# Finer sum pieces, two helper buffers, and sums of group 1 of the second pass in a free bank, in a graph network kernel on one core

## What is computed

```python
# layer 0, a gated cell; layer 1, two neighbour means
msg = h[src] @ W_msg.T + b_msg + edge_embed[clip(edge_type)]
messages = segment_sum(msg, dst, num_segments=3125)
x = layernorm(x + gru_cell(messages, x, W_ih, W_hh, b_ih, b_hh))
def sage(h, w_self, w_neigh, b):
    neigh = segment_sum(h[src], dst) / maximum(deg, 1)
    return h @ w_self + neigh @ w_neigh + b
h = relu(sage(x, w_self1, w_neigh1, b1))
x = layernorm(x + sage(h, w_self2, w_neigh2, b2))
```

## Time and profile before

| | us |
|---|---|
| median of three runs | 766.2 |
| profiled execution, its own time | 764.69 |
| span of its instructions | 762.9 |
| counting stage, from the start of the tiles to the verdict | about 15 to 412 |
| first pass | about 414 to 516 |
| second pass | about 516 to 650 |
| third pass | about 650 to 763 |

### The profile page before, as it was taken

The page is one execution under the profiler, slowest core; times in us unless marked ns, Lnnn a source line. Parts: engine busy times, 40 slices in busy tenths (PEclk is TensorE's granted clock), DMA queues, the critical chain, the costliest instruction groups (busy, mean ns, idle before and its releaser), DMA issues.

```text
span 762.9 us, 14609 instructions
## 1 busy us (share of the span) xinstructions
PE 662.5 (87%) x3061; PEld 311.9 (41%) x3061; DVE 468.4 (61%) x1469; ACT 244.3 (32%) x486; POOL 171.0 (22%) x342
## 2 busy tenths in 40 slices
PE   2767899989888899888766999948999999999995
PEld 0222344434333343333222544413555456666663
DVE  7789999998888879999894357651010010034434
ACT  3044444332422235656664245531111221100000
POOL 2432333232222235445340012230100111100000
PEclk9879999999999999999998999989999999999998
DMA  5000000000000000000002011000100110211210
GB/s 155 1 1 0 1 1 1 0 1 0 1 0 1 0 1 1 0 1 0 0 0 81 16 28 55 16 30 29 42 25 17 41 41 29 87 43 43 69 31 16
DMA packets 29437, 17.32 MB, mean 23 GB/s; under 512 B 1841, under 2 KB 28223, under 8 KB 29400
## 3 DMA queue, kind: packets, MB, share of 16 engines
q1 hardware_dynamic: 29400, 16.82, 7.6%
HBM read 10.38 MB, written 6.44 MB: 22 GB/s over the span
## 4 chain that ended last, share of the span: by engine, by line
PE 64%; DVE 18%; issue 7%; DVEq 5%; ACT 2%; DMA 1%; SPq 0%; POOL 0%; ACTq 0%
PE PS L917 14%; PE PS L994 11%; PE PS L1232 11%; PE PS L873 10%; DVE S L619 10%; DVE D L613 3%; PE PS L1161 3%; PE PS L1055 2%; PE PS L1196 2%; DVEq L619 2%; PE PS L895 1%; PE PS L1150 1%; PE PS L1149 1%; PE PS L1028 1%; PE PS L1029 1%
## 5 line engine op out<-in xcount | busy, mean ns | idle before, releaser
L917 PE MATMUL PS<-S,D 128*128 128x449 bf16 x780 | 219.0, 368 | 53.8 <-DVE S L619 45.4
L619 DVE TENSOR_SCALAR S<-iota_h,src_col,src_w 128x440 bf16<-128x440 f16 x749 | 253.1, 399 | 0.2 <-issue 0.2
L472 POOL COPY S<-T 128x27 bf16 (+1 forms) x262 | 113.5, 434 | 236.4 <-PE PS L917 222.2
L917 PEld LDWEIGHTS PS<-S,D 128*128 128x128 bf16 x780 | 75.7, 97 | 193.6 <-DVE S L619 152.3
L1275 ACT ACTIVATE AT<-digits 128x1152 uint8 (+5 forms) x75 | 77.1, 1029 | 160.7 <-DVE digits L608 160.7
L613 DVE TENSOR_TENSOR D<-iota_t,dst 128x384 bf16<-128x384 f16 x260 | 93.8, 361 | 33.3 <-PE PS L917 32.1
L873 PE MATMUL PS<-AT,xp 128*128 128x512 bf16 x375 | 91.3, 379 | 0.0
L994 PE MATMUL PS<-AT,x1p 128*128 (+2 forms) x450 | 86.8, 353 | 0.0
L1232 PE MATMUL PS<-xp,AT 128*128 128x384 bf16 (+1 forms) x525 | 85.6, 326 | 0.0
L1232 PEld LDWEIGHTS PS<-xp,AT 128*128 (+2 forms) x525 | 51.5, 98 | 33.9 <-issue 0.3
L994 PEld LDWEIGHTS PS<-AT,x1p 128*128 128x128 bf16 x450 | 39.5, 99 | 44.0 <-issue 2.3
(11 more groups left out here) (167 smaller groups left out, 628.8 us busy)
## 6 DMA issues: line engine op xcount, KB each, us to landing
slot<-x_rows SPq DMA_DIRECT2D x12, 256.0 KB, 2.9
xstage<-x SPq DMA_DIRECT2D x6, 256.0 KB, 4.9
x_rows<-slot SPq DMA_DIRECT2D x6, 256.0 KB, 2.2
y_rows<-slot SPq DMA_DIRECT2D x6, 256.0 KB, 2.2
res_rows<-slot SPq DMA_DIRECT2D x6, 256.0 KB, 2.2
slot<-res_rows SPq DMA_DIRECT2D x6, 256.0 KB, 3.1
out_rows<-slot SPq DMA_DIRECT2D x6, 256.0 KB, 2.2
slot<-xT SPq DMA_DIRECT2D x3, 256.0 KB, 2.6
```

What stands on the lines that cost most here:

```text
L472: g.tensor_copy(S[:, where:where + V, SPAN:WIDE], T[:, :, ds(c0 + where, V)].rearrange("p k c -> p c k")).then_inc(sem("types_placed"), 1)
L619: v.tensor_scalar(S[:, u, 0:SPAN], iota_h[:, :], src_col[:, ds(c0 + u, 1)], src_w[:, ds(c0 + u, 1)], ALU.is_equal, ALU.mult).then_inc(sem( ...
L917: mm(PS[:, par, 0:WIDE], ring[:, u, :], S[:, u, 0:WIDE], start=opens and u == 0, stop=last).then_inc(sem("tiles_summed" if last else "item ...
```

## The change

Four things are changed.

1. `LEAST` becomes a table of five runs (2 for tiles 0 to 8, 3 for 9 to 15, 4 for 16 to 18, 5 for 19 to 22, 12 for 23 and 24; before: 2 up to tile 20, 4 from there). In `count_tile` the passes 1 to `LEAST - 2` are written out ahead of the loop, each with a piece between its halves and one behind it. So a tile has `2 * (LEAST - 2) + 3` pieces: 3, 5, 7, 9 and 23. The plan holds all 125 steps, so none is left behind the last tile.
2. `apart` has two halves that take turns (in rows 0 to 15 of the last tile's columns of `AT`, which are written later), and `last_rows` no longer waits for its own `Relu` at the end of each round.
3. `p2_second` sums group 1 of the second pass in PSUM bank 2: six row blocks ahead of `rows_back(6)`, the rest behind it and behind the rest of `p2_first`. What the first step of the second pass did between the shares of that sum is now written out ahead of `p2_step(2)`, and `second(0)` and `hidden(1)` stand inside `p2_step(2)`. `chunk_inputs(0)` uses bank 0. ACT and DVE have their parts in the same new order.
4. The DMA that brings group 0's rows back into `slot[2]` is issued in the first pass, ahead of the last store.

```diff
@@ constants
-PIECES = 3
-LEAST = 2
-LEAST_WIDE = 4
+LEAST_RUNS = ((0, 9, 2), (9, 16, 3), (16, 19, 4), (19, 23, 5), (23, 25, 12))
+LEAST = tuple(n for lo, hi, n in LEAST_RUNS for _ in range(lo, hi))
-EARLY_PLAN = (0,) * 7 + (4, 4, 5, 4, 5, 4, 5, 7, 5, 7, 7, 7, 8, 10, 9, 9, 10, 10)
+EARLY_PLAN = (0,) * 7 + (3, 3, 5, 3, 5, 3, 5, 6, 5, 6, 6, 6, 8, 9, 10, 11, 18, 13)
+    apart = AT[:, 0:16, (TILES - 1) * P:(TILES - 1) * P + SPAN // 8]
@@ SP, first pass
+                if q == NC:
+                    sp.wait_ge(sem("p1_y"), NC + 1)
+                    sp.wait_ge(sem("p1_x1_out"), 16)
+                    sp.dma_start(slot[2][:, :].rearrange("p (t f) -> p t f", f=F),
+                                 x1_dram[0:512, :].rearrange("(t p) f -> p t f", p=P)).then_inc(sem("p2_x1_in"), 16)
                 x1_store(q)
@@ PE, count_tile
                 early_piece(t, 0)
...
+                single = LEAST[t] - 2
+                pieces = 2 * single + 3
+                early_piece(t, 0, pieces)
+                for i in range(1, single + 1):
+                    one_pass(first + t + i, first + i, D, i - 2 if is_dense(t) and i >= 3 else None, between_halves=lambda: early_piece(t, 2 * i - 1, pieces))
+                    early_piece(t, 2 * i, pieces)
+                    if t == TILES - 1 and i == 2:
                         turn_tile(t - 1)
...
+                with pe.Fori(single + 1, more) as i:
+                    one_pass(first + t + i, first + i, D, i - 2 if is_dense(t) else None)
+                early_piece(t, pieces - 2, pieces)
+                one_pass(first + t + more, first + more, D, None, closes=True, between_halves=lambda: early_piece(t, pieces - 1, pieces))
@@ PE, end of the first pass
+                if q == NC:
+                    p2_second(0, 6)
                 rows_back(q)
+            p2_second(6, 20)
             p2_first(20, TILES - 1)
+            p2_second(20, TILES - 1)
@@ PE, second pass
+            p2_close(0)
             degrees(0, 512)
             chunk_inputs(0, 512)
+            p2_close(1)
+            hidden(0, 512)
+            degrees(1, 512)
+            chunk_inputs(1, 512)
...
+                if isinstance(q, int) and q == 2:
+                    agg("p2", x1p, q, w, [delayed, rest, lambda: second(1, 512)])
+                else:
+                    agg("p2", x1p, q, w, [inputs, lambda: None, lambda: second(q - 1, 512)])
@@ ACT, last_rows
-                    a.activation(apart[:, :], iota_h[:, :], ACT.Abs, scale=-1.0, bias=src_col[:, ds(c, 1)]).then_inc(sem(f"apart_set{t}"), 1)
+                    near = apart[:, ds((b & 1) * 8, 8), :]
+                    a.activation(near, iota_h[:, :].rearrange("p (a n) -> p a n", a=8), ACT.Abs, scale=-1.0,
+                                 bias=src_col[:, ds(c, 1)]).then_inc(sem(f"apart_set{t}"), 1)
...
-                    act.wait_ge(sem(f"S_last_set{t}"), i - 2)
```

More of the change, by code:

```diff
@@ L183, in graph_kernel @@
     src_w = place(r, "src_w", [P, CP], fp32)
-    apart = place(r, "apart", [P, SPAN], bf16)
     assert r[0] <= Z_at + 15 * F * 4
@@ L289, in second_rows, with sum_bank @@
             return PS[0:rows, 3:5, :].rearrange("p b (h w f) -> p (b h) w f", h=2, w=2)[:, 0:k, which, :]
+        def sum_bank(q):
+            return q + 1 if isinstance(q, int) and q < 2 else 0
         def s_at(q):
@@ L800, in mean_neighbours @@
                 dve.wait_ge(sem("p2_agg"), q + 1)
-                v.tensor_tensor(nT, nT, PS[:, 1 if isinstance(q, int) and q == 0 else 0, 0:w], ALU.mult).then_inc(sem("p2_n"), 1)
+                v.tensor_tensor(nT, nT, PS[:, sum_bank(q), 0:w], ALU.mult).then_inc(sem("p2_n"), 1)
             def residual(q, last):
@@ L812, in _ @@
             mean_neighbours(0, 512)
-            with dve.Fori(1, NC) as q:
+            mean_neighbours(1, 512)
+            residual(0, False)
+            with dve.Fori(2, NC) as q:
                 mean_neighbours(q, 512)
@@ L882, in early_steps, with early_piece @@
                         early_sum(q, j0, j1)
-            def early_piece(t, n):
-                pieces = PIECES + 2 if is_dense(t) else PIECES
+            def early_piece(t, n, pieces):
                 n0, steps = EARLY_BEGIN[t], EARLY_PLAN[t]
@@ L1093, in p2_first, with p2_second @@
                 pe.nop()
+            def p2_second(j0, j1):
+                pe.wait_ge(sem("p1_c"), NC + 1)
+                pe.wait_ge(sem("p1_low"), -(-j1 // 4))
+                with pe.If(general):
+                    pe.nop()
+                with pe.Else():
+                    for j in range(j0, j1):
+                        for s in range(PARTS):
+                            mm(PS[:, 2, :], x1p[:, j, s, :], AT[:, j, 512:1024], start=(j == 0 and s == 0), stop=False)
+                pe.nop()
             fills = {0: (lambda: late_sum(NC, 0, TILES), lambda: late_sum(NC - 1, 0, 4)),
@@ L1125, in chunk_inputs @@
             def chunk_inputs(q, w):
-                bank = 2 if isinstance(q, int) and q == 0 else 1
+                bank = 0 if isinstance(q, int) and q == 0 else 1
                 if bank == 1:
@@ L1180, in inputs, with delayed, rest @@
                     chunk_inputs(q, w)
-                agg("p2", x1p, q, w, [inputs, lambda: None, lambda: second(q - 1, 512)])
-            p2_step(1, 512)
-            with pe.Fori(2, NC) as q:
+                def delayed():
+                    second(0, 512)
+                    hidden(1, 512)
+                def rest():
+                    degrees(q, w)
+                    chunk_inputs(q, w)
+                if isinstance(q, int) and q == 2:
+                    agg("p2", x1p, q, w, [delayed, rest, lambda: second(1, 512)])
+                else:
+                    agg("p2", x1p, q, w, [inputs, lambda: None, lambda: second(q - 1, 512)])
+            p2_step(2, 512)
+            with pe.Fori(3, NC) as q:
                 p2_step(q, 512)
@@ L1461, in inputs_out @@
                 act.wait_ge(sem("p2_h_sum"), 2 * q)
-                a.activation(slot[3][:, 0:w], PS[:, 2 if isinstance(q, int) and q == 0 else 1, 0:w], ACT.Copy).then_inc(sem("p2_x1c"), 1)
+                a.activation(slot[3][:, 0:w], PS[:, 0 if isinstance(q, int) and q == 0 else 1, 0:w], ACT.Copy).then_inc(sem("p2_x1c"), 1)
             def relu_rows(q, w):
@@ L1480, in _ @@
             inputs_out(0, 512)
-            with act.Fori(1, NC) as q:
+            act.wait_ge(sem("p2_agg"), 1)
+            stage_sums("p2", 1)
+            relu_rows(0, 512)
+            inputs_out(1, 512)
+            second_out(0, False)
+            with act.Fori(2, NC) as q:
                 relu_rows(q - 1, 512)
```

46 lines of the change are left out of this document (16 added, 30 removed).

## The result

The changed kernel takes 735.75 us in the median of four runs (734.35 to 736.11), the kernel before, timed beside it, 766.59 us (four runs, 764.7 to 769.02): a ratio of 0.959 with a 95% interval of 0.956 to 0.962. The profiled execution has a span of 733.9 us, 29.0 less than before. The forecast was 733.9 us, with a range of 726 to 746.

What follows compares the result with a forecast made beforehand. The prediction took DVE to bound the counting stage and PE the second pass. Terms 18.8 + 4.4 + 3.1 + 6.0 = 32.3 us off the profiled 764.7 gave 732.4; 1.5 more for the median made 733.9, range 726 to 746.

Steps and rivals of the forecast that it cites:

- Finer pieces, tiles 9 to 23: Counting stage: nearly every piece cut to one step, so DVE waits less for PE; 18.8 us, bounds 9.4 and 27.8.
- ACT's helper, tile 24: Tile 24's helped batches: without ACT's wait for its own Relu, DVE sets the pace; 4.4 us, bounds 0 and 5.6.
- Behind the last tile: After tile 24: fifteen leftover matmuls go and the last pass ends earlier, so digits start sooner; 3.1 us, bounds 1.8 and 3.7.
- Group 1's sum in bank 2: Between the passes: 75 matmuls move from the second pass into PE's idle time; 6.0 us, bounds 3 and 8.4.
- The early load: Ahead of the second pass: loading slot[2] early removes a 1.95 us DMA wait, counted within the moved sum's 6.0 us.
- I leave 0.3 for each of the 20 changes from tile 4 on: Counting stage: DVE's wait for PE assumed to remain at each change from one tile to the next, 6.0 us in all.
- the 1 us that was named as the bound of being wrong: Tiles 21 to 23: waits of more than 1 us between written-out passes would make the prediction wrong.
- Slower: Counting stage: loading code for 37 more written-out passes holds PE and so DVE; up to 798 us, chance 0.03.
- Pieces only move the waits: Counting stage: PE is late in the written-out passes, gaining 9.4 us in place of 18.8; 743 us, chance 0.18.
- The helper loop isn't ACT's wait: Tile 24 keeps its 2.33 us round, as DVE, PE and ACT are locked in one ring; 737.5 us, chance 0.1.
- the moved sum gives little: Between the passes: new waits for DVE are longer than reckoned, gaining 3 us for 6; 737 us, chance 0.09.
- More than forecast: Counting stage: the waits left at the tiles' changes vanish as well; 727 us, chance 0.08.

Runs made afterwards that it cites:

- e9: Changed kernel with tile 20's digits moved to tile 23, spread steps, 18 plus six zero products, later ACT help in tile 24: 732.31 us, beside the unaltered changed kernel's 733.89.
- e1: Kernel before with only the LEAST table, written-out passes, new plan and finer pieces: 745.38 us, ratio 0.973.
- e4: Kernel before with only the LEAST table and written-out passes, pieces and plan as before: 765.85 us, ratio 0.9996.
- e11: Changed kernel with no steps around tile 23's closing pass, its 18 steps in the other 21 pieces: one time of 738.12 us.
- e6: Changed kernel with tile 20's digits taken at the start of tile 23 instead of in tile 22: 733.5 us, ratio 0.9605.
- e7: Changed kernel with another plan, 5, 5, 9 and 16 steps in tiles 10, 12, 22 and 23: 734.93 us, ratio 0.961.
- e2: Kernel before with only apart in two halves and no wait of ACT for its own Relu: 761.81 us, ratio 0.9945.
- e8: Changed kernel with the load of slot[2] back at its old place behind p1_done: one time of 733.9 us.
- e12: Changed kernel with ACT's help in tile 24 from the fourth batch on, DVE making the third's sixth row: 735.47 us, ratio 0.960.
- e3: Kernel before with only group 1's second-pass sum in bank 2 and the early load of slot[2]: 758.1 us, ratio 0.990.

## Why the prediction was right

Predicted 733.9, measured 735.75 and, beside e9, 733.89. That the second meets the forecast to the hundredth is luck. The gain in the medians was 30.8 and 30.9 us, and 29.0 between the first two profiled executions, where the sum says 32.3; and the 1.5 us that were added for the median over a profiled execution did not come (735.75 against 735.67). The terms of the sum, in us:

| term | predicted | measured |
|---|---|---|
| *Finer pieces, tiles 9 to 23* | 18.8 | 16.5 |
| *ACT's helper, tile 24* | 4.4 | 4.0 |
| *Behind the last tile* | 3.1 | 3.0 |
| *Group 1's sum in bank 2* and *The early load* | 6.0 | 7.3 |
| clock behind the last tile | not foreseen | -2.1, or 0 |
| up to tile 4, behind `hidden(1)` | not foreseen | 0.3 |

- **Finer pieces.** The mechanism is shown: e1 has it alone with the full 16.4 us, e4 has the same straight code without the finer pieces and gains nothing. What was mis-sized is "I leave 0.3 for each of the 20 changes from tile 4 on": the 21 starts of tiles 4 to 24 hold 9.3 us and not 6.0. At the starts of tiles 4 to 20, where DVE takes digits between `D_again` and its next `D`, 0.19 to 0.44 stay; tiles 23 and 24 have no digits there, and each keeps the 1.3 us that it had before. At tile 24 moving the steps takes nothing off it (e11), at tile 23 digits do (e6). Tiles 21 and 22 keep 0.77 and 0.63 at their starts, which no run explains. Inside tiles 21 to 23 another 1.6 us stay, where 3.0 were allowed for tiles 22 and 23. The largest, 0.88 in tile 22, is under the 1 us that was named as the bound of being wrong; it stands behind a piece of two steps in the middle of the tile, while the prediction says that at most the last piece of a tile has two, and e7 removes it with two steps fewer. Two of the signs did not come: DVE's waits are 12.2 us and not near 9, and the largest is 1.31 and not under 1.
- **ACT's helper.** The round fell to DVE's pace as foreseen, the form of 55 elements costs nothing, and ACT's late start stayed (1.31 us; 1.2 were left for it). But the 4.0 us are not the helper's alone: by itself it gives 2.3 (e2), the finer pieces by themselves 1.3 (e1), and 0.4 need both. The working took the span of fourteen helped batches as one rate; only the last eight ran at 2.33 us. So the size came out right in part by luck: the finer pieces removed other waits in the same tile, which the working had put on the helper.
- **Behind the last tile** is right in both its parts. 2.9 of the 3.0 us come with the finer pieces (e1).
- **Group 1's sum in bank 2.** The waits came as worked out: 0.27 for 0.45, and 1.17 for 1.2 (DVE's "1.85 in all" is 0.42 + 0.69 + 0.69 = 1.80, which takes 0.05 off both). Too high was "about 0.25 us each" for four new blocks with branches: the trace has no gap there. With that 1.0 and 0.2 the 5.8 of the working (of which "6.0" was made) come to 7.0, against 7.3. The early load, counted with them, gives nothing (e8). The 1.7 us for the clock depend on the execution: in e2 the second pass's first share ran in 5.99 us with the kernel's old order, the low clock having fallen on the matmuls ahead of it, and from the transposes of group 5 to `hidden(1)` it took 47.4 us where before had 49.2 and e4 50.1. So this term is 5 to 8 us, by which execution with the old order one takes.
- **The clock.** Not foreseen at all. Behind the last tile PE waits for the verdict, before and after (4.2 us), falls to the lower level in that wait and stays there for about 7 or about 14 us. The profile of before has 7, the changed kernel's first one 14 and its second 7, at 90.3 and 92.4 us from the verdict to group 5. Both lengths occur with either order: of the four profiled executions that end the counting stage as before, one has the long one (e4), and of the eight that end it as the change does and have no products, five (e1, the first profile after, e7, e11, e12). One and the same kernel shows both, so the length is not fixed by the order of work; whether the change makes the long one likelier, these few don't tell, and what sets it stays open.
- **The rivals.** *Slower*, by code loading, is out: e4 holds all written-out passes and has the time of before. The queue that brings instructions moved 28 packets, before 24, and the rows show no wait for it. The Trainium skill, "Advanced Engine Details and Errata", section ISA Cache, gives lines of 16 KB, two of them, and beside that 128 KB for TensorE, which the prediction leaves out; that straight code could stall PE was the prediction's conclusion from it, and no run here bears it out. *Pieces only move the waits* is out, as 16.5 us are gained where it had 9.4. *The helper loop isn't ACT's wait* is out by the 2.06 us of e2, *the moved sum gives little* by the 7.1 of e3 where it had 3. *More than forecast* (727) is out, since the tiles' starts keep 9.3 us.

## What to carry to other kernels

Filler work on an engine that hands buffers back cost here by the size of its pieces and hardly by its amount (tiles 22 and 23 took ten more steps for 0.4 us): cut it to what the consumer's own half batch covers, and put more places in the code for it, even by writing loops out. Before counting on "no wait left", find the bare round trip between the two engines: what stays there falls only if the waiting engine has work of its own to put in it. Work that fills an idle stretch belongs ahead of the wait in program order and must end before it does; behind the wait it is on the path.
